# The last expert's rows read back and written plainly in place of accumulated: an attention and mixture-of-experts kernel on one core

## The chip, the cores and the metric

The kernel runs on one core of a Trainium2 chip. The metric is device time in microseconds (us), lower is better. Five engines work side by side: TensorE (PE in the profile, PEld its weight loads), VectorE (DVE), ScalarE (ACT), GpSimd (POOL) and SyncE (SP). Each runs its own instruction stream and waits for the others by semaphores. DMAs are issued here by SyncE and by GpSimd. A PSUM bank holds 128 x 512 float32; DMA can't read one, so results leave a bank through ScalarE or VectorE.

## The reference

```python
def _L0_ffn_ref(hidden_states, gate_weight, gate_up_proj, down_proj):
    ...
    probs = jax.nn.softmax(router_logits.astype(jnp.float32), axis=-1)
    top_v, top_i = jax.lax.top_k(probs, top_k)
    top_v = top_v / top_v.sum(axis=-1, keepdims=True)
    combine_w = jnp.einsum('tke,tk->te', jax.nn.one_hot(top_i, num_experts, dtype=top_v.dtype), top_v).astype(x.dtype)
    def expert_step(acc, inp):
        gu, dp, w = inp
        gate, up = jnp.split(x @ gu.T, 2, axis=-1)
        hidden = jax.nn.silu(gate) * up
        y = hidden @ dp.T
        return (acc + w[:, None] * y, None)
    ...
x = x + _L0_xattn_ref(_layernorm(x, axis=-1), mask_BxSx4224_bf0, ctx_2048, ctx_2048, ...)
x = x + _L0_ffn_ref(_layernorm(x, axis=-1), ...)
```

x has 8 x 112 tokens of 512 numbers. After an attention block each token goes to two of 8 experts with inner width 1024, and the weighted outputs of its two experts are added to it.

## The kernel before, in words

The first 185 us do the attention of the 8 batches in four pairs, write the sum x2 = x + attention to `out`, normalise it, choose two experts for each token and scatter each token's normalised row, with its weight and its number, into a list for each expert in DRAM (`slots`, 256 rows of 514 numbers an expert, unused rows zero). The scatter is an indirect write on GpSimd (L1327): 112 rows of 2,056 bytes, the destination rows given by a column of indices.

Then come the experts, one after another, two to an iteration `it` of a loop (three iterations, then the fourth unrolled with `more=False`). For an expert, `xe` holds its list of 256 rows, and its inner width is done in 8 units of 128. For each unit TensorE does the gate and up products (L412, L413; the last unit in a shorter form, L230 to L234), ScalarE and VectorE form silu(gate) * up and split it into a high and a low part, and TensorE adds the unit's share of the down product (`pe_down`, L498) into two banks `YB[e]` that hold the 256 rows as two halves: SC0 and SC1 for an even expert, R and T2 for an odd one. After the eighth unit the sum is whole, which TensorE signals for each half by `y_mm`.

An expert's output takes this way. ScalarE (`y_out`, L814) multiplies each half by the rows' weights (column D of `xe`) into `ys`, signal `y_ok`. GpSimd (`send_y`, L1362) sends each half by an indirect write with `compute_op=ALU.add`: the DMA adds the 128 rows of 2,048 bytes to rows of `out`. The indices `yidx` are made by VectorE from column D + 1 of `xe` (L1174, L1176, signal `yidx_ok`), in the fifth unit of the expert; unused rows go to spare rows behind the real ones. Between experts GpSimd (`add_y`) waits for both landings (`y_added`) and then sets a flag (`y_free`, L1276) that lets ScalarE write `ys` again. So the adds of one expert never meet those of another.

The kernel can hold longer lists: behind the eighth expert every engine loads the length of the longest list (`value_load`) and skips a large body of code if it is at most 256 (`CAP`). In the profiled execution it is skipped by every engine. On VectorE this test stands directly behind its last operation for the eighth expert (L1220, L1221), on ScalarE behind `y_out` of the last expert (L880, L881), on GpSimd between the seventh expert and the last (L1378, L1379), on TensorE behind its last product (L633, L634), on SyncE behind its last load (L1508). After the body GpSimd does `send_y(NE - 1, 1)` for the eighth expert, and SyncE waits for all of `y_added` (L1536). L45 is not a line of the kernel: it is the end of the program, where every engine has a DRAIN and a handshake.

Of the kernel before, what the change touches and what calls it, by code (L numbers as in the profile page):

```python
# [4 lines left out]
F32 = mybir.dt.float32  # L5
# [5 lines left out]
ALU = mybir.AluOpType  # L11
# [4 lines left out]
D = 512  # L16
# [6 lines left out]
NE = 8  # L23
# [3 lines left out]
ROUNDS = 4  # L27
# [13 lines left out]
def build_kernel(nc, x, ctxT, ctxn, w_all, gwt, units, out):  # L41
# [3 lines left out]
    with stack:  # L45
        def sem(name):
            return stack.enter_context(nc.semaphore(name))
# [6 lines left out]
        def at(name, shape, dt, offset):  # L54
            return nc.alloc_sbuf_tensor_at(name, shape, dt, offset=offset)
# [7 lines left out]
        def sb(name, shape, dt):  # L63
            offset = top[0]
            top[0] += size(shape, dt)
            return at(name, shape, dt, offset)
# [14 lines left out]
        yidx = sb("yidx", [128, 2, 2], I32)  # L81
# [63 lines left out]
        o_e = top[0]  # L145
# [7 lines left out]
        o_l = top[0]  # L153
# [14 lines left out]
        xe = [at(f"xe{n}", [128, 2, RW], F32, o_s + n * 4128) for n in range(2)]  # L168
# [13 lines left out]
        ys = at("ys", [128, 2, D], F32, o_e)  # L182
        hh = [at(f"hh{n}", [128, CAP], F32R, o_e + 4096 + n * 1024) for n in range(2)]
        hl = [at(f"hl{n}", [128, CAP], F32R, o_e + 6144 + n * 1024) for n in range(2)]


        T = [pb(f"T{n}") for n in range(3)]
# [206 lines left out]
        gu_mm, silu_ok, h_ok = sem("gu_mm"), sem("silu_ok"), sem("h_ok")  # L394
        y_mm, y_ok, yidx_ok = sem("y_mm"), sem("y_ok"), sem("yidx_ok")
        y_added, y_free = sem("y_added"), sem("y_free")
        UB = 2 * IT

        LG = 3
# [7 lines left out]
        YB = [[SC[0], SC[1]], [R, T[2]]]  # L407
# [66 lines left out]
        def pe_gu_short(pe, it, u):  # L474


            e = u // IT
            pe.wait_ge(u_lo, it * UB + u + 1)
            wh, wl = uh[u % GU], ul[u % GU]
            for w in range(2):  # L480
                hl_matmul(GB[u % 2][w][:, 0:CAP],
                          lambda k: wh[:, w * D + 128 * k:w * D + 128 * k + 128],
                          lambda k: wl[:, w * D + 128 * k:w * D + 128 * k + 128],
                          lambda k: eh[e][:, k, :], lambda k: el_[e][:, k, :], KT).then_inc(gu_mm if w else g_mm, 1)

        def pe_gu(pe, it, u):
            e = u // IT
            pe.wait_ge(u_lo, it * UB + u + 1)
            if u % IT == 0:
                pe.wait_ge(e_lo, 2 * (2 * it + e) + 2)  # L490
            wh, wl = uh[u % GU], ul[u % GU]
            for w in range(2):
                for k in range(KT):
                    c = slice(w * D + 128 * k, w * D + 128 * k + 128)
                    last = gu_product(GB[u % 2][w], wh[:, c], wl[:, c], eb[e], k)
                last.then_inc(gu_mm if w else g_mm, 1)

        def pe_down(pe, it, u):  # L498
            i = u % IT
            pe.wait_ge(h_ok, it * UB + u + 1)  # L500
            if u == IT:
# [13 lines left out]
        def pe_experts(pe, it, more=True):  # L515


            for u in range(1, UB + 1):
                e, i = u // IT, u % IT
                if u == UB - 1 and not more:  # L520
                    pe_gu_short(pe, it, u)
                elif u < UB:
                    pe_gu(pe, it, u)
# [121 lines left out]
        def _(act):  # L645
# [195 lines left out]
            def experts(it, more=True):  # L841

                for u in range(1, UB + 1):
                    e, i = u // IT, u % IT
                    if u == UB - 1 and not more:
                        silu_short(it, u)
                    elif u < UB:
                        silu(it, u)
                        if more or u + LG < UB:
                            hi_u(it, u + LG)  # L850
                    elif more:
                        silu(it + 1, 0)
                        hi_u(it + 1, LG)
                    if (i == 4 or i == 6) and (more or e == 0):
                        hi_e(2 * (2 * it + e + 1) + 1 + i // 6, (e + 1) % 2, i // 6, YB[(e + 1) % 2][i // 6])
                    if i == 0:
                        y_out(it, e - 1)

            for p in range(PAIRS):
# [19 lines left out]
            act.wait_ge(most_ok, 1)  # L879
            longest = act.value_load(mosti[0:1, 0:1], min_val=0, max_val=TOK)  # L880
            with act.If(longest > CAP):  # L881
                for u in range(LG):
                    hi_u(NE // 2, u)
                hi_e(2 * NE + 1, 0, 0, YB[0][0])
                hi_e(2 * NE + 2, 0, 1, YB[0][1])
                silu(NE // 2, 0)
                hi_u(NE // 2, LG)
                with act.Fori(NE // 2, ROUNDS * NE // 2 - 1) as j:
                    experts(j)
                experts(ROUNDS * NE // 2 - 1, more=False)  # L890

        @block.vector
        def _(dve):
            v = nc.vector
# [272 lines left out]
            def experts(it, more=True):  # L1167
                for u in range(UB):
                    e, i = u // IT, u % IT
                    b = u % 2  # L1170
                    if i == 4:
                        if e == 0:
                            dve.wait_ge(xe_in[0], 16 * (it + 1))
                        link(v.scalar_tensor_tensor(yidt[:, e, :], xe[e][:, :, D + 1], 0.0, padid[:, :],  # L1174
                                                    ALU.is_equal, ALU.mult))
                        v.scalar_tensor_tensor(yidx[:, e, :], xe[e][:, :, D + 1], -1.0, yidt[:, e, :],  # L1176
                                               ALU.add, ALU.add).then_inc(yidx_ok, 1)
                    if u == UB - 1 and not more:
                        dve.wait_ge(gu_mm, it * UB + u + 1)
                        dve.wait_ge(silu_ok, it * UB + u + 1)  # L1180
                        link(v.tensor_tensor(hf[b][:, :], GB[b][1][:, 0:CAP], hs[b][:, :], ALU.mult))
                    else:
                        dve.wait_ge(u_copy, it * UB + u + 1 - short[0])
                        link(v.tensor_tensor(us[b][:, :], GB[b][1][:, 0:CAP], us[b][:, :], ALU.add))
                        dve.wait_ge(silu_ok, it * UB + u + 1)
                        link(v.tensor_tensor(hf[b][:, :], us[b][:, :], hs[b][:, :], ALU.mult))  # L1186
                    link(v.tensor_copy(hh[b][:, :], hf[b][:, :]))
                    v.tensor_tensor(hl[b][:, :], hf[b][:, :], hh[b][:, :].bitcast(F32), ALU.subtract)\  # L1188
                        .then_inc(h_ok, 1)
                    if more or u + LG < UB:  # L1190
                        lo_u(it, u + LG)
                    if u + 1 < UB:
                        if more or u + 2 < UB:
                            sum_g(it, u + 1)
                    elif more:
                        sum_g(it + 1, 0)
                    if (i == 4 or i == 6) and (more or e == 0):
                        lo_e(2 * (2 * it + e + 1) + 1 + i // 6, (e + 1) % 2, i // 6, YB[(e + 1) % 2][i // 6])
# [22 lines left out]
            with dve.If(longest > CAP):  # L1221
                for u in range(LG):
                    lo_u(NE // 2, u)
                lo_e(2 * NE + 1, 0, 0, YB[0][0])
                lo_e(2 * NE + 2, 0, 1, YB[0][1])
                sum_g(NE // 2, 0)
                looped(NE // 2, ROUNDS * NE // 2 - 1, experts)
                experts(ROUNDS * NE // 2 - 1, False)

        @block.gpsimd  # L1230
        def _(pool):
# [130 lines left out]
            def send_y(n, e):  # L1362
                pool.wait_ge(yidx_ok, n + 1)
                for t in range(2):
                    pool.wait_ge(y_ok, 2 * n + 1 + t)
                    pool.indirect_dma_start(out[:, :], bass.IndirectOffsetOnAxis(yidx[:, e, t:t + 1], 0),  # L1366
                                            ys[:, t, :], None, compute_op=ALU.add).then_inc(y_added, 16)

            def add_y(n, e):
                send_y(n, e)  # L1370
                pool.wait_ge(y_added, 32 * n + 32)
                signal(y_free)

            pool.wait_ge(x2_out, 16 * NB + 16 * 2)
            for n in range(NE - 1):
                add_y(n, n % 2)
            pool.wait_ge(most_ok, 1)
            longest = pool.value_load(mosti[0:1, 0:1], min_val=0, max_val=TOK)  # L1378
            with pool.If(longest > CAP):  # L1379
                for n in range(NE - 1, ROUNDS * NE - 1):  # L1380
                    add_y(n, n % 2)

                pool.wait_ge(yidx_ok, ROUNDS * NE)
                pool.wait_ge(y_ok, 2 * ROUNDS * NE)

            send_y(NE - 1, 1)

        @block.sync
        def _(sp):
# [184 lines left out]
```

## Time and profile before

| | |
|---|---|
| runs without the profiler | 456.36, 456.49, 456.56 us; median 456.49 |
| the profiled execution | 456.27 us, of which the span from the first to the last instruction is 454.5 |
| mean granted TensorE clock | 0.994 |
| busy: TensorE, its loads, VectorE, ScalarE, GpSimd | 441.0, 373.3, 343.8, 253.5, 98.7 us |
| instructions | 7156 |
| DMA | 88.39 MB, mean 194 GB/s |

A page of the profile gives each engine's busy time; "idle before" names what ended the idle time. Register, branch, semaphore and DMA-issuing instructions don't count as busy, and stand under an engine's name with a q (DVEq, POOLq). For an indirect DMA, GpSimd is shown busy while it generates the descriptors; the bytes move later. "DMA to landing" runs from the start of that instruction to the last increment of its semaphore. All times are from the span's start.

### The profile page before, as it was taken

The page shows a single profiled execution, that of the slowest core. Times are in us where ns is not written, and L with a number is a line of the kernel's source. Part 1 is how long each engine was busy: PE and PEld are TensorE (multiplying, and loading weights), DVE is VectorE, ACT ScalarE, POOL GpSimd, SP SyncE. Part 2 cuts the span into 40 slices and gives each one's busy share as a digit, 9 for nine tenths or more (in the row PEclk, how much of TensorE's full clock was granted, in tenths as well). Part 3 has the DMA queues.
Part 4 walks back from the last instruction along what each step waited for, and adds up shares of the span by engine and source line. Part 5 has one row for each costly group of instructions (what it writes and reads, how often), then busy time and mean ns, then how long its engine had stood idle before and what let it go on. Part 6 is the DMA issues. An engine that isn't in the chain of part 4 may idle for free.

```text
span 454.5 us, 7156 instructions
## 1 busy us (share of the span) xinstructions
PE 441.0 (97%) x2530; PEld 373.3 (82%) x2530; DVE 343.8 (76%) x644; ACT 253.5 (56%) x414; POOL 98.7 (22%) x128
## 2 busy tenths in 40 slices
PE   8999999999999999999999999999999999999991
PEld 6979888878888678888888888888888888888880
DVE  5867546556645678898988988988988888888850
ACT  4566434514623666666566566666666656656621
POOL 6060071334427253003003003003003003003002
PEclk9999999999999999999999999999999999999997
DMA  8996984434545465976766856856956846856203
GB/s 274 349 259 186 278 216 139 142 51 140 195 115 226 129 224 153 341 236 194 249 199 176 272 185 199 263 165 205 276 156 204 276 157 198 284 164 196 56 0 51
DMA packets 26911, 88.39 MB, mean 194 GB/s; under 512 B 2560, under 2 KB 8704, under 8 KB 26880
## 3 DMA queue, kind: packets, MB, share of 16 engines
q1 hardware_dynamic: 23296, 80.13, 54.4%
q0 software_dynamic: 3584, 7.88, 8.7%
q8 instruction: 16, 0.26, 0.3%
q14 instruction: 15, 0.12, 0.1%
HBM read 73.55 MB, written 14.45 MB: 194 GB/s over the span
## 4 chain that ended last, share of the span: by engine, by line
PE 85%; DVE 4%; DMA 3%; ACT 2%; issue 2%; POOL 1%; SPq 1%; POOLq 0%; ACTq 0%; DVEq 0%
PE T L412 13%; PE PJ L412 13%; PE PJ L413 6%; PE T L413 6%; PE SC L509 3%; PE SC L510 3%; PE SC L511 3%; PE T L245 3%; PE PJ L232 2%; PE PJ L234 2%; PE PJ L233 2%; PE SC L262 2%; PE SC L266 2%; PE SC L264 2%; DMA wTs<-in_weights 2%
## 5 line engine op out<-in xcount | busy, mean ns | idle before, releaser
L897 DVE TENSOR_TENSOR ul<-ng,uh 128x1536 fp32r<-128x1536 f32 x64 | 112.5, 1757 | 3.1 <-ACT uh L647 1.9
L647 ACT ACTIVATE uh<-ng 128x1536 fp32r<-128x1536 f32 x64 | 94.8, 1481 | 0.3 <-DMA ng<-in_units 0.3
L412 PE MATMUL T<-eb,uh 128*128 128x512 f32 x248 | 88.7, 397 | 0.0
L412 PE MATMUL PJ<-eb,uh 128*128 128x512 f32 x248 | 88.7, 397 | 0.0
L1366 POOL DMA_INDIRECT out<-ys,yidx x16 | 27.8, 1738 | 194.3 <-ACT ys L821 191.8
L413 PE MATMUL PJ<-eb,ul 128*128 128x256 f32 x248 | 69.7, 281 | 0.0
L413 PE MATMUL T<-eb,ul 128*128 128x256 f32 x248 | 69.6, 281 | 0.0
L412 PEld LDWEIGHTS PJ<-eb,uh 128*128 128x128 f32 x248 | 46.6, 188 | 11.2
L412 PEld LDWEIGHTS T<-eb,uh 128*128 128x128 f32 x248 | 46.6, 188 | 11.2
L413 PEld LDWEIGHTS T<-eb,ul 128*128 128x128 f32 x248 | 46.8, 189 | 1.3
L413 PEld LDWEIGHTS PJ<-eb,ul 128*128 128x128 f32 x248 | 46.7, 188 | 1.3
L1289 POOL TENSOR_TENSOR vl<-vs,vh 128x512 fp32r<-128x512 f32 (+1 forms) x24 | 30.6, 1308 | 8.0 <-DVE xr L992 5.4
L647 ACT ACTIVATE us<-PJ 128x256 f32<-128x256 f32 x32 | 12.3, 384 | 31.5 <-PE PJ L413 31.4
L1186 DVE TENSOR_TENSOR hf<-us,hs 128x256 f32<-128x256 f32 x63 | 26.8, 425 | 3.0 <-ACT hs L839 1.1
L1188 DVE TENSOR_TENSOR hl<-hf,hh 128x256 fp32r<-128x256 f32 x64 | 27.2, 425 | 2.2
L839 ACT ACTIVATE hs<-gs 128x256 f32<-128x256 f32 x63 | 25.9, 412 | 4.0 <-DVE gs L1165 3.9
L647 ACT ACTIVATE us<-T 128x256 f32<-128x256 f32 x31 | 11.9, 384 | 28.4 <-PE T L413 28.4
L509 PE MATMUL SC<-uh,hh 128*128 128x512 f32 x64 | 25.9, 405 | 0.0
L510 PE MATMUL SC<-ul,hh 128*128 128x512 f32 x64 | 25.2, 393 | 0.0
L511 PE MATMUL SC<-uh,hl 128*128 128x512 f32 x64 | 25.1, 392 | 0.0
L647 ACT ACTIVATE gs<-PJ 128x256 f32<-128x256 f32 x32 | 12.2, 382 | 23.0 <-PE PJ L413 22.0
L1327 POOL DMA_INDIRECT slots<-xr,idx x16 | 17.5, 1095 | 18.8 <-issue 17.3
(240 smaller groups left out, 918.5 us busy)
## 6 DMA issues: line engine op xcount, KB each, us to landing
ng<-in_units SPq DMA_DIRECT2D x64, 768.0 KB, 4.5
vs<-in_ctxn SPq DMA_DIRECT2D x8, 768.0 KB, 5.2
kTs<-in_ctxT SPq DMA_DIRECT2D x8, 750.0 KB, 5.0
slots<-zero SPq DMA_DIRECT2D x8, 514.0 KB, 12.9
xe<-slots SPq DMA_DIRECT2D x8, 514.0 KB, 4.3
wTs<-in_weights SPq DMA_DIRECT2D x8, 512.0 KB, 8.0
out<-x_all SPq DMA_DIRECT2D x8, 224.0 KB, 3.9
x_all<-in_x SPq DMA_DIRECT2D x1, 896.0 KB, 19.0
```

What stands on the lines that cost most here:

```text
L412: nc.tensor.matmul(o[:, :].rearrange("p (h s) -> p h s", h=2), wh, both[:, k, :, :], start=k == 0, stop=False)
L413: return nc.tensor.matmul(o[:, 0:CAP], wl, both[:, k, 0, :], start=False, stop=k == KT - 1)
L509: nc.tensor.matmul(o, hh[b][:, s], wh, start=i == 0, stop=False)
L510: nc.tensor.matmul(o, hh[b][:, s], wl, start=False, stop=False)
L511: last = nc.tensor.matmul(o, hl[b][:, s], wh, start=False, stop=i == IT - 1)
L647: nc.scalar.activation(o, i, ACT.Copy).then_inc(s, 1)
L839: nc.scalar.activation(hs[b][:, :], gs[b][:, :], ACT.Silu).then_inc(silu_ok, 1)
L897: v.tensor_tensor(o, whole, hi.bitcast(F32), ALU.subtract).then_inc(s, 1)
L1186: link(v.tensor_tensor(hf[b][:, :], us[b][:, :], hs[b][:, :], ALU.mult))
L1188: v.tensor_tensor(hl[b][:, :], hf[b][:, :], hh[b][:, :].bitcast(F32), ALU.subtract)\
L1289: g_.tensor_tensor(vl[a][0:n, j, :], vs[a][0:n, j, :], vh[a][0:n, j, :].bitcast(F32), ALU.subtract).then_inc(v_lo, 1)
L1366: pool.indirect_dma_start(out[:, :], bass.IndirectOffsetOnAxis(yidx[:, e, t:t + 1], 0), ys[:, t, :], None, compute_op=ALU.add).then_inc(y_ ...
```

## The change

VectorE takes over the last expert's output. GpSimd reads the rows of `out` that this expert adds to into a new tile `so_far`, once the seven others are added and the indices are there. VectorE computes bank x weight + `so_far` into `ys`, and GpSimd writes the rows by two indirect writes without `compute_op`. ScalarE's `y_out` of the eighth expert moves into the skipped body. If the body runs, it reads `so_far` again at its own end.

```diff
+        so_far = at("so_far", [128, 2, D], F32, o_e + 8192)
...
+        far_in, last_ok = sem("far_in"), sem("last_ok")
...
-                    if i == 0:
+
+                    if i == 0 and (more or e == 1):
                         y_out(it, e - 1)
...
             with act.If(longest > CAP):
+                y_out(NE // 2 - 1, 1)
...
                 experts(ROUNDS * NE // 2 - 1, False)
+                dve.wait_ge(far_in, 64)
+                dve.wait_ge(y_mm, 2 * ROUNDS * NE)
+
+            dve.wait_ge(far_in, 32)
+            for t in range(2):
+                dve.wait_ge(y_mm, 2 * NE - 1 + t)
+                v.scalar_tensor_tensor(ys[:, t, :], YB[1][t][:, :], xe[1][:, t, D:D + 1], so_far[:, t, :],
+                                       ALU.mult, ALU.add).then_inc(last_ok, 1)
...
+            def read_far(n):
+
+                pool.wait_ge(yidx_ok, n)
+                for t in range(2):
+                    pool.indirect_dma_start(so_far[:, t, :], None, out[:, :],
+                                            bass.IndirectOffsetOnAxis(yidx[:, 1, t:t + 1], 0)).then_inc(far_in, 16)
+
             pool.wait_ge(x2_out, 16 * NB + 16 * 2)
             for n in range(NE - 1):
                 add_y(n, n % 2)
+            read_far(NE)
             pool.wait_ge(most_ok, 1)
             longest = pool.value_load(mosti[0:1, 0:1], min_val=0, max_val=TOK)
             with pool.If(longest > CAP):
+                pool.wait_ge(far_in, 32)
                 for n in range(NE - 1, ROUNDS * NE - 1):
                     add_y(n, n % 2)
-
-                pool.wait_ge(yidx_ok, ROUNDS * NE)
-                pool.wait_ge(y_ok, 2 * ROUNDS * NE)
-
-            send_y(NE - 1, 1)
+                read_far(ROUNDS * NE)
+
+            for t in range(2):
+                pool.wait_ge(last_ok, t + 1)
+                pool.indirect_dma_start(out[:, :], bass.IndirectOffsetOnAxis(yidx[:, 1, t:t + 1], 0),
+                                        ys[:, t, :], None).then_inc(y_added, 16)
```

VectorE's listing ends so before the change; L1181 to L1188 are the last unit's work of the eighth expert, and the last row is the jump over the body, which itself stands above these rows in a second copy of the same lines.

```order
L1184 TENSOR_TENSOR us_181<-PJ,us_181 128x256 [waits u_copy]
L1186 TENSOR_TENSOR hf_159<-us_181,hs_157 128x256 [waits silu_ok,vchain]
L1187 CAST hh_184<-hf_159 128x256 [waits vchain]
L1188 TENSOR_TENSOR hl_186<-hf_159,hh_184 128x256 [waits vchain]
L1181 TENSOR_TENSOR hf_160<-T,hs_158 128x256 [waits silu_ok,gu_mm]
L1187 CAST hh_185<-hf_160 128x256 [waits vchain]
L1188 TENSOR_TENSOR hl_187<-hf_160,hh_185 128x256 [waits vchain]
L1221 UNCONDITIONAL_BRANCH
```

With the change it ends so, the lines being 6 higher from there on.

```order
L1192 TENSOR_TENSOR hf_159<-us_181,hs_157 128x256 [waits silu_ok,vchain]
L1193 CAST hh_184<-hf_159 128x256 [waits vchain]
L1194 TENSOR_TENSOR hl_186<-hf_159,hh_184 128x256 [waits vchain]
L1187 TENSOR_TENSOR hf_160<-T,hs_158 128x256 [waits silu_ok,gu_mm]
L1193 CAST hh_185<-hf_160 128x256 [waits vchain]
L1194 TENSOR_TENSOR hl_187<-hf_160,hh_185 128x256 [waits vchain]
L1227 UNCONDITIONAL_BRANCH [waits y_mm,far_in]
L1241 SCALAR_TENSOR_TENSOR ys<-R,xe_156,so_far 128x512 [waits y_mm,far_in]
L1241 SCALAR_TENSOR_TENSOR ys<-T,xe_156,so_far 128x512 [waits y_mm]
L45 UNCONDITIONAL_BRANCH
```

The two new rows stand behind the end of the skipped body. The test itself (COMPARE_AND_BRANCH) is row 503 of the listing in both kernels, and the body ends at row 786 or 787: some 284 rows are jumped over. On ScalarE they are 173, on TensorE some 750.

GpSimd, from the seventh expert's writes to the test, before the change:

```order
L1366 DMA out<-ys,yidx 1152x512 [waits y_ok,yidx_ok]
L1366 DMA out<-ys,yidx 1152x512 [waits y_ok]
L1276 MEMSET flags 1x1 [waits y_added]
L1378 TENSOR_LOAD mosti [waits most_ok]
L1378 ISA x2
L1379 COMPARE_AND_BRANCH
```

and with it:

```order
L1380 DMA out<-ys,yidx 1152x512 [waits y_ok,yidx_ok]
L1380 DMA out<-ys,yidx 1152x512 [waits y_ok]
L1290 MEMSET flags 1x1 [waits y_added]
L1392 DMA so_far<-out,yidx 128x512 [waits yidx_ok]
L1392 DMA so_far<-out,yidx 128x512
L1400 TENSOR_LOAD mosti [waits most_ok]
L1400 ISA x2
L1401 COMPARE_AND_BRANCH
```

Two gathers have come between the seventh expert's flag and the test, behind a wait for the eighth expert's indices.

## Rows read from the trace of the kernel before

**Rows 1.** The page: busy us (share of the span) and instructions of each engine.

```profile
PE 441.0 (97%) x2530; PEld 373.3 (82%) x2530; DVE 343.8 (76%) x644; ACT 253.5 (56%) x414; POOL 98.7 (22%) x128
```

**Rows 2.** Timeline from 443.9: start us, us, engine, line, operation [idle before <-releaser].

```profile
443.99 0.39 PE L511 MATMUL R<-uh,hl 128*128 128x512 f32 x1
...
444.48 0.69 ACT L821 ACTIVATE ys<-R,xe 128x512 f32<-128x512 f32 x1 [3.31 <-PE R L511]
...
445.11 0.69 ACT L821 ACTIVATE ys<-T,xe 128x512 f32<-128x512 f32 x1
445.95 1.56 POOL L1366 DMA_INDIRECT out<-ys,yidx  x1 [21.39 <-ACT ys L821]
447.81 1.54 POOL L1366 DMA_INDIRECT out<-ys,yidx  x1 [0.30 <-issue]
```

**Rows 3.** The chain of waits, its last piece: start us, us, what.

```profile
447.51 1.85 POOLq L45
```

**Rows 4.** L1366 from 445 to 455, the last expert's two writes.

```profile
DMA to landing us min/median/max: 4.7/4.9/5.1
```

**Rows 5.** L45 by engine: duration ns min/median/max, first and last start us.

```profile
L45 POOLq DRAIN  x1: 8093/8093/8093, 446.2 to 446.2; - x1
...
L45 SPq COMPARE_BRANCH  x1: 38/38/38, 452.9 to 452.9; - x1
...
L45 ACTq DRAIN  x1: 81/81/81, 446.4 to 446.4; - x1
...
L45 DVEq DRAIN  x1: 65/65/65, 446.7 to 446.7; - x1
```

**Rows 6.** L981 on VectorE: an SBUF tile added to a bank.

```profile
L981 DVE TENSOR_TENSOR x_all<-PJ,x_all x7: 680/691/692, 48.6 to 157.3; 112x512 f32<-112x512 f32 x7
```

**Rows 7.** The jumps over the body: VectorE, TensorE, ScalarE.

```profile
L1221 DVEq COMPARE_BRANCH  x1: 63/63/63, 443.9 to 443.9; - x1
...
L634 PEldq COMPARE_BRANCH  x1: 3561/3561/3561, 444.3 to 444.3; - x1
...
L881 ACTq COMPARE_BRANCH  x1: 54/54/54, 445.9 to 445.9; - x1
```

**Rows 8.** VectorE's loop branch, and the operation behind it in the timeline.

```profile
L1203 DVEq COMPARE_BRANCH  x3: 50/56/72, 239.3 to 377.3; - x3
...
239.76 0.42 DVE L1165 TENSOR_TENSOR gs<-PJ,gs 128x256 f32<-128x256 f32 x1
```

**Rows 9.** L1327, plain indirect writes: one at 169.6 with its landing; four from 147.1.

```profile
L1327 POOL DMA_INDIRECT slots<-xr,idx x1: 1068/1068/1068, 169.6 to 169.6; - x1
...
DMA to landing us min/median/max: 3.4/3.4/3.4
...
L1327 POOL DMA_INDIRECT slots<-xr,idx x4: 937/942/1056, 147.1 to 150.9; - x4
...
DMA to landing us min/median/max: 3.9/4.8/5.1
```

**Rows 10.** L1460 on SyncE, direct plain writes of zeros to out, 161.8 and 162.3.

```profile
DMA to landing us min/median/max: 2.6/2.8/3.1
```

**Rows 11.** The last indices (L1176); GpSimd's timeline behind expert seven; landing of its writes.

```profile
L1176 DVE SCALAR_TENSOR_TENSOR yidx<-xe,yidt x8: 160/161/161, 188.9 to 429.7; 128x2 int32<-128x2 f32 x8
...
418.37 1.66 POOL L1366 DMA_INDIRECT out<-ys,yidx  x1 [0.30 <-issue]
424.47 0.09 POOL L1276 MEMSET flags<- 1x1 f32 x1 [4.45 <-DMA out<-ys,yidx]
...
DMA to landing us min/median/max: 6.1/6.5/6.9
```

**Rows 12.** All of L1327; landings of all of L1366; SyncE's last loads.

```profile
L1327 POOL DMA_INDIRECT slots<-xr,idx x16: 937/944/2215, 85.8 to 174.7; - x16
...
DMA to landing us min/median/max: 4.7/8.5/10.7
...
L1447 SPq DMA_DIRECT2D ng<-in_units x3: 328/328/328, 407.8 to 416.7; - x3
```

More of the change, by code:

```diff
@@ L184, in build_kernel @@
         hl = [at(f"hl{n}", [128, CAP], F32R, o_e + 6144 + n * 1024) for n in range(2)]
+        so_far = at("so_far", [128, 2, D], F32, o_e + 8192)
+        assert o_e + 12288 <= o_l
         T = [pb(f"T{n}") for n in range(3)]
```

## Prediction

> **What bounds the kernel now.** I read the page first: TensorE is busy 441.0 of 454.5 us [rows 1], so until its last product nothing that this change touches can matter unless it holds TensorE up. Then I looked at what happens after that product, in the timeline of the end [rows 2]. The last product into R starts at 443.99, ScalarE scales R into the first half of ys at 444.48 and T into the second at 445.11 (0.69 each). GpSimd generates the first accumulating write at 445.95 (1.56 us) and the second at 447.81 (1.54 us). The chain of waits ends in GpSimd's queue at L45, the end of the program [rows 3]. The issue-to-landing times of the two writes are 4.7 and 5.1 us [rows 4], so the first lands at 450.6 and the second at 447.81 + 5.1 = 452.9. At L45 [rows 5], SyncE's wait for the landing is over at 452.9, but GpSimd's DRAIN lasts from 446.2 for 8.093 us, to 454.3, and is the last thing to end: 1.4 us behind the landing, 4.9 us behind the end of the second generation (449.35). The tail from the scaled ys to the end of the span is thus a bit over 9 us, and it is all that the change can shorten.
>
> **The change part by part.** The sum is made against the profiled execution, whose span is 454.5 and whose time is 456.27; the median of the three runs shown is 456.49, so a change of the span is added to that median.
>
> *Who scales the last rows.* ScalarE's two ys instructions of the last expert go, two of VectorE come (bank times weight plus so_far). The nearest row is VectorE's add of a bank and an SBUF tile, 112x512, 690 ns [rows 6]; ScalarE took 687 ns [rows 2]. So the operation itself is worth 0. ScalarE has nothing else to do there.
>
> *When VectorE can start.* This is the term that decides. The new instructions stand behind VectorE's test on the longest list. It already exists: the branch at L1221 starts at 443.9 [rows 7], before R is complete. But it is taken over the whole overflow body, 284 rows of the listing, and VectorE's next instruction behind it, the DRAIN at L45, starts only at 446.7 [rows 5]. It waits for nothing that the trace shows, and ScalarE's own DRAIN, behind the same sort of test but a shorter body, starts 0.5 us behind its branch (445.9 to 446.4) [rows 5, 7]. So I read 446.7 - 443.9 = 2.8 us as the price of the long jump. In the changed kernel the first instruction behind the jump is the one that everybody waits for: it starts at about 446.8, not at 444.48. That costs **+2.3 us**. The bounds: 0.3 to 0.5 us of delay from the branches that go on quickly (VectorE's loop branch at 239.3, whose next operation runs at 239.76 [rows 8], and ScalarE's); and 3.6 us from TensorE's branch at L634, which starts at 444.3 and is shown 3561 ns long [rows 7]. I take 2.8, because it is this engine's jump over this body. From the quick end the start is bound by R, at 444.5, and the term is 0; from the slow end it is 443.9 + 3.6 + 0.1 = 447.6, +3.1.
>
> *The hand-over.* ScalarE's first half ends at 445.17 and GpSimd starts at 445.95, 0.78 us later. The same wait stands in the new kernel for last_ok: 0. The first write is then issued at 446.8 + 0.69 + 0.78 = 448.3. VectorE's second half ends at about 448.15, before GpSimd is free for it.
>
> *Generating the writes.* From the first generation to the second the accumulating ones took 447.81 - 445.95 = 1.86 us. A plain indirect write of 112 rows took 1.07 us as the first of its batch and 0.94 in the median of four [rows 9]; with the 0.30 us between two of them that is 1.36 instead of 1.86, **-0.5 us**. Bounds: 0.94 + 0.3 (-0.6), and no gain at all (0), if 128 rows cost as an accumulating write does.
>
> *From the second generation to its landing.* It was 5.1 us. The plain indirect write that ran alone landed 3.4 us behind its issue, those of a batch of four beside loads in 3.9 to 5.1 [rows 9]; two direct plain writes of 256 KB each landed in 2.6 to 3.1 [rows 10]. At the end of the program nothing else runs, and the first write will be all but through when the second is generated, so I take a value close to the lone one, 3.5: **-1.6 us**. Bounds: 2.6 (-2.5) and 4.5 (-0.6). The Trainium skill, "DMA: Bandwidth & Descriptors", section "Anatomy of one DMA — SWDGE (gpsimd) path", fits such a transfer by 2.0 us plus bytes over 436 GB/s; for 262,144 bytes that is an estimate of 2.6 us, and the sum by it would be 0.9 us lower than mine. The lone plain write of 112 rows, a smaller one, needed 3.4 here, so the trace speaks against it.
>
> *The end.* GpSimd's DRAIN ends 1.4 us behind the landing, as now: 0.
>
> *The reading back.* Two gathers, 256 KB each, come on GpSimd's queue. Behind which wait? They need the indices of the last expert, which VectorE writes at 429.7 [rows 11], and nothing is queued behind them but the test and the last two writes. GpSimd had put the seventh expert's flag at 424.47 [rows 11] and was idle from there to 445.95. There is no gather in this trace; the dearest indirect DMA of any sort took 2.2 us to generate, and the slowest landing, of an accumulating one, was 10.7, with a median of 8.5 [rows 12]. With 430.0 + 2.2 + 0.3 + 10.7 the rows are there by 443.2, and by 441 with the median landing. VectorE wants them at 446.8. At the cheap end they cost nothing either. The loads of the experts' weights are over by then (SyncE issues the last at 416.7 [rows 12]), so they disturb no transfer and are not disturbed. GpSimd's own test, now right behind 424.5, moves behind the gathers, to about 434; even with 3.6 us for its jump it is waiting by 438. If this cover were gone, each microsecond that so_far is late would be one on the end. 0. Releasing ys: with the last expert written by VectorE, the wait for y_free at its head goes; it was long satisfied.
>
> **The sum**: +2.3 - 0.5 - 1.6 = +0.2 us. 456.49 + 0.2 = **456.7 us**. The change does what it should (the writes are cheaper by 2.1 us), and the jump takes it back. Its own range: the landing's bounds alone give -0.7 to +1.2, the slow end of the stall alone +1.0, a stall of half the size -1.2. That is 455.3 to 457.7.
>
> **The rivals.**
>
> *A, VectorE goes on at once.* The 2.8 us could belong to the DRAIN or to the end of the program and not to the jump, so that the new instructions run when R is ready, at 444.5. For it: the loop's branches cost 0.3 to 0.5 us [rows 8]. Against it: ScalarE's DRAIN at the same L45 came at once, TensorE's branch shows 3.6 us of its own. Then the first term is 0: -0.5 - 1.6 = -2.1, **454.4 us**, faster. The Trainium skill, "Runtime: NRT & Kernel Launch", section "Instruction fetch mechanics", says that a taken branch stalls only if its target lies outside a window of two pages of 256 instructions, and forces the fetch of a page otherwise. A target 284 rows on may lie in such a window, in which case this rival would be right; ScalarE's 173 rows cost 0.5 us and agree with the rule, and VectorE's 2.8 speaks for the other side of it.
>
> *B, slower: GpSimd's DRAIN counts from the last generation, not from the landing.* It ended 4.9 us behind the end of the second generation and 1.4 us behind the landing, and this trace has only this one, so it can't tell which. SyncE's wait was over at 452.9, and the DRAIN is what the span ended on. If what it does behind the last generation takes 4.9 us whatever lands, the cheaper landing is worth nothing. The second generation then ends at 448.3 + 1.36 + 1.0 = 450.7 instead of 449.35, **+1.3 us, 457.8 us**. It decides as soon as those 4.9 us end later than the landing and its 1.4, which here is so for any landing quicker than 4.5 us behind the issue. Against it: in the loop the flag of the seventh expert is set at 424.47, and its second write, issued at 418.37, lands 6.1 us later, at 424.47 as well [rows 11]; so GpSimd is free for the next thing long before 4.9 us are over, and a DRAIN that asks for the landed state of the queues is the plainer reading.
>
> *C, the change doesn't do what it says:* the gathers or GpSimd's test come so late that the last writes wait for so_far. It needs a landing beyond 446.8, 14 us behind the second gather's issue; the slowest in the trace is 10.7. By that it would be 457 to 460.
>
> **How the numbers follow.** A difference of 0.2%, 0.9 us, is about what a measurement of this kernel can tell from none. The forecast gets 0.62 (0.50 within 0.2%, 0.04 faster with a stall of half the size or less, 0.08 slower with TensorE's stall or a landing of 4.5). A gets 0.16, all faster. B gets 0.18, 0.16 of it slower and 0.02 within. C and the like get 0.04, slower. So 0.20 faster, 0.52 the same, 0.28 slower. The range takes in the forecast's own, a stall of half the size (-1.2, 455.3) and B: 455.0 to 457.9. Left out are A and C.
>
> **What would show it.** In the changed profile: VectorE's first scalar_tensor_tensor starts near 446.8, 2.8 us behind its branch, and TensorE's last product near 444 as before; the two so_far gathers start near 430 and land before 443; GpSimd's last two writes start at 448.3 and 449.6, take 1.0 us each and land in 3.4 to 3.6; the DRAIN ends 1.4 us behind the landing. A start at 444.5 makes A right, a DRAIN that ends 4.9 us behind the last generation B. The forecast is wrong also if the plain writes of 128 rows to out take as long as the accumulating ones: then it is +2.3.

## The result, and the profile after

The changed kernel takes 455.16 us in the median of 22 runs, the kernel before 456.26 us in the median of its runs beside them; the ratio is 0.998, with a 95% interval of 0.9971 to 0.999. So it is faster by 0.2%, a little over 1 us. The profiled execution is at 455.30 us with a span of 453.5, 1.0 us less than before. I had forecast 456.7, and no difference, from a sum of +0.2 us. Two terms of the sum, both of which I had carried over from a row that stood near, were too dear by 0.5 and 0.8 us; the others came within 0.1 us. One execution each of e10 (734.05 us) and of e12 (546.96 us), far off the others, is left out of their ratios.

The timeline of the end, to be read beside [rows 2] (start us, us, engine, line, operation, idle before and what ended it):

```profile
443.93 0.40 PE L515 MATMUL R<-uh,hl 128*128 128x512 f32 x1
...
446.81 0.75 DVE L1241 SCALAR_TENSOR_TENSOR ys<-R,xe,so_far 128x512 f32<-128x512 f32 x1 [3.52 <-issue]
447.48 0.74 DVE L1241 SCALAR_TENSOR_TENSOR ys<-T,xe,so_far 128x512 f32<-128x512 f32 x1
447.85 0.99 POOL L1409 DMA_INDIRECT out<-ys,yidx  x1 [15.34 <-DVE ys L1241]
449.14 0.98 POOL L1409 DMA_INDIRECT out<-ys,yidx  x1 [0.30 <-issue]
```

R is complete as early as before, but VectorE starts on it only at 446.81. The idle time is not put down to an engine or a DMA ("issue"), and the chain of waits shows where it lies, between the branch and the next wait:

```profile
443.80 0.06 DVEq L1227
443.86 2.87 issue
446.73 0.02 DVEq L1240
```

At L45, answering to [rows 5], and the landings of L1409, answering to [rows 4]:

```profile
L45 POOLq DRAIN  x1: 5047/5047/5047, 448.3 to 448.3; - x1
L45 SPq COMPARE_BRANCH  x1: 38/38/38, 451.9 to 451.9; - x1
...
DMA to landing us min/median/max: 2.7/3.0/3.2
```

GpSimd's DRAIN ends at 453.3, 1.4 us behind SyncE's wait for the landing, just as before, and it is still the last thing to end. The reading back is where it was meant to be:

```profile
L1392 POOL DMA_INDIRECT so_far<-out,yidx x2: 1018/1070/1122, 430.1 to 431.4; - x2
```

Term by term; the first two columns are from the profiled executions, in us, and the last two say by how much the change moves the end:

| | before | changed | change, forecast | change, measured |
|---|---|---|---|---|
| the scaling starts | 444.48 | 446.81 | +2.3 | +2.33 |
| one half takes | 0.69 | 0.75 | 0 | +0.06 |
| its end to the first write's start | 0.78 | 0.28 | 0 | -0.50 |
| first write to second | 1.86 | 1.30 | -0.5 | -0.56 |
| second write to its landing | 5.1 | 2.7 | -1.6 | -2.4 |
| landing to the DRAIN's end | 1.4 | 1.4 | 0 | 0 |
| sum | | | +0.2 | -1.1 |

### The profile page after: what moved, and what is told of

Its sections match the earlier page's. It is cut to its first block, busy times and chain, and to the rows that moved or that the text cites. A ratio compares the mean times of both kernels' runs of the same rounds, so it can differ in the third digit from the quotient of the medians.

```text
span 453.5 us, 7157 instructions
## 1 busy us (share of the span) xinstructions
PE 441.0 (97%) x2530; PEld 373.4 (82%) x2530; DVE 345.8 (76%) x646; ACT 251.9 (56%) x412; POOL 99.8 (22%) x130
## 4 chain that ended last, share of the span: by engine, by line
PE 85%; DVE 5%; issue 3%; DMA 2%; ACT 2%; POOL 1%; POOLq 0%; DVEq 0%
PE T L416 13%; PE PJ L416 13%; PE PJ L417 6%; PE T L417 6%; PE SC L513 3%; PE SC L514 3%; PE SC L515 3%; PE T L248 3%; PE PJ L235 2%; PE PJ L237 2%; PE PJ L236 2%; PE SC L265 2%; PE SC L269 2%; PE SC L267 2%; DMA slots<-xr,idx 2%
## 5 line engine op out<-in xcount | busy, mean ns | idle before, releaser
L1380 POOL DMA_INDIRECT out<-ys,yidx x14 | 24.7, 1766 | 171.5 <-ACT ys L825 169.3
L1190 DVE TENSOR_TENSOR us<-PJ,us 128x256 f32<-128x256 f32 x32 | 13.6, 424 | 10.9 <-ACT us L651 10.9
```

## The experiments

Ratios are to the kernel before, measured beside each; the changed kernel's is 0.998.

**e1: VectorE's results ahead of its test.** They go to a tile of their own, `fin`, which the two last writes now send, so that the skipped body, if it runs, can make them again.

```diff
+        fin = at("fin", [128, 2, D], F32, o_e + 12288)
...
+            def finish(read, made):
+                dve.wait_ge(far_in, read)
+                for t in range(2):
+                    dve.wait_ge(y_mm, made - 1 + t)
+                    v.scalar_tensor_tensor(fin[:, t, :], YB[1][t][:, :], xe[1][:, t, D:D + 1], so_far[:, t, :],
+                                           ALU.mult, ALU.add).then_inc(last_ok, 1)
+
+            finish(32, 2 * NE)
             longest = dve.value_load(mosti[0:1, 0:1], min_val=0, max_val=TOK)
             with dve.If(longest > CAP):
...
+                finish(64, 2 * ROUNDS * NE)
...
             with pool.If(longest > CAP):
-                pool.wait_ge(far_in, 32)
+                pool.wait_ge(last_ok, 2)
...
                 read_far(ROUNDS * NE)
+                pool.wait_ge(last_ok, 4)
```

> VectorE's two new instructions stand ahead of its test on the longest list, and write a tile of their own (fin), so nothing is jumped over before them; if the body runs it computes them again. Theory (the 2.9 us between branch and first new instruction are the price of the jump over the body): the first starts when R is complete, about 444.5 instead of 446.8, GpSimd's first write about 445.6 instead of 447.8, and the time falls 2.2 to 2.4 us below the changed kernel's 455.2, to about 452.9. Rival (the instructions wait for something else that comes at 446.8, the rows read back or the banks): the start stays at 446.8 and the time at 455.2.

Measured: 454.02 us, ratio 0.9942 (0.9923 to 0.9961). The timeline:

```profile
444.49 0.75 DVE L1232 SCALAR_TENSOR_TENSOR fin<-R,xe,so_far 128x512 f32<-128x512 f32 x1 [1.14 <-PE R L516]
...
445.52 0.99 POOL L1413 DMA_INDIRECT out<-fin,yidx  x1 [12.96 <-DVE fin L1232]
446.82 0.98 POOL L1413 DMA_INDIRECT out<-fin,yidx  x1 [0.31 <-issue]
```

The start is at 444.49, released by TensorE, so the 2.3 us were the jump's, and both writes go 2.3 us earlier. But the time fell by 0.4%, some 1.7 us, and in the profiled execution (455.2 us, the slowest of its nine) the span is 453.4, hardly less than the changed kernel's. The landing says why:

```profile
DMA to landing us min/median/max: 3.3/4.1/5.0
```

The second write took 5.0 us again instead of 2.7. A write's landing is told in 16 increments of its semaphore, which I read as one share for each of the core's 16 DMA engines. Of the second write's 16 shares 15 had told of their landing by 449.55; the last did at 451.77. This opened a question that the prediction hadn't asked, and e5, e6 and e12 go after it.

**e2: one wait at the write instead of two.** The kernel before, with a tiny memset that takes the wait for the indices.

```diff
             def send_y(n, e):
                 pool.wait_ge(yidx_ok, n + 1)
+                if n == NE - 1:
+                    signal(rest_ready)
```

> The kernel before, with one tiny GpSimd memset between the wait for the last indices and the last expert's first write, so that the write has only one wait left (for ys). Theory (GpSimd starts an indirect DMA 0.28 us behind a signal when that is the DMA's only wait, and 0.78 when a separate wait instruction stands ahead of it): first write 0.5 us earlier, about 445.45, time 0.5 us below the kernel before. Rival (0.28 against 0.78 lies in who signals, VectorE or ScalarE, or in the accumulating form): the write still starts 0.78 behind ScalarE's end and the time is unchanged.

```profile
444.99 0.69 ACT L822 ACTIVATE ys<-T,xe 128x512 f32<-128x512 f32 x1
445.32 1.56 POOL L1369 DMA_INDIRECT out<-ys,yidx  x1 [15.43 <-ACT ys L822]
```

ScalarE's first half starts at 444.36 and ends at 445.05; the write starts 0.28 us later, although ScalarE signals and the write accumulates. So the hand-over is a matter of the waits at the DMA and not of who signals: with two, one of them stands as an instruction of its own (L1365 in the kernel before) and the DMA is dispatched only behind it. In the trace the whole 0.5 us is there. The time is 456.53, ratio 0.9995 (0.998 to 1.001), too wide an interval to show 0.1%; that the 0.5 us reach the end is read from the profiled spans alone, 453.9 against 454.5.

**e3: the changed kernel, its last writes still accumulating.** What was read back is then counted twice.

```diff
-                                        ys[:, t, :], None).then_inc(y_added, 16)
+                                        ys[:, t, :], None, compute_op=ALU.add).then_inc(y_added, 16)
```

> The changed kernel with compute_op=ALU.add left on its last two writes, so the last expert's rows of the output are counted twice over. Theory (the plain form alone saves 0.56 us between the generations and 2.4 us from the second issue to the landing): 2.9 us slower than the changed kernel, 458.1, each generation about 1.55 us, landing of the second 5.1 behind its issue, hand-over still 0.28. Rival (the landing was quicker because it fell later, in a quieter time): within 0.6 us of 455.7. And GpSimd's DRAIN: if it follows the landing it ends 1.4 us behind it, if it follows the generation it ends 3.2 us behind the second generation, as in the changed kernel.

Measured: 458.81 us, ratio 1.0041 (1.0023 to 1.0059), 0.6% or 2.8 us above the changed kernel. The generations:

```profile
448.79 1.61 POOL L1409 DMA_INDIRECT out<-ys,yidx  x1 [15.52 <-DVE ys L1241]
450.70 1.57 POOL L1409 DMA_INDIRECT out<-ys,yidx  x1 [0.30 <-issue]
```

and the landings and the end:

```profile
DMA to landing us min/median/max: 4.9/5.0/5.2
...
L45 POOLq DRAIN  x1: 8097/8097/8097, 449.2 to 449.2; - x1
L45 SPq COMPARE_BRANCH  x1: 38/38/38, 455.9 to 455.9; - x1
```

The form alone is worth what the theory said (2.9 us), and the hand-over of 0.28 stays (448.51 to 448.79). The DRAIN ends at 457.3, 1.4 us behind the landing but 5.0 behind the second generation's end, where the changed kernel had 3.2: it follows the landing.

**e4 and e10: a shorter body to jump over.** e4 leaves the last unrolled iteration out of VectorE's skipped body (188 rows of the listing are left), e10 nearly all of it (4 rows are left).

```diff
                 sum_g(NE // 2, 0)
                 looped(NE // 2, ROUNDS * NE // 2 - 1, experts)
-                experts(ROUNDS * NE // 2 - 1, False)
                 dve.wait_ge(far_in, 64)
```

```diff
-                lo_e(2 * NE + 1, 0, 0, YB[0][0])
-                lo_e(2 * NE + 2, 0, 1, YB[0][1])
-                sum_g(NE // 2, 0)
-                looped(NE // 2, ROUNDS * NE // 2 - 1, experts)
-                experts(ROUNDS * NE // 2 - 1, False)
                 dve.wait_ge(far_in, 64)
```

> The changed kernel with the last unrolled iteration of VectorE's skipped body left out (lists over 256 are no longer handled; the body doesn't run with these inputs). The jump goes over some 190 rows of the listing instead of 284, near ScalarE's 173 that cost 0.5 us. Theory A (it is the distance that costs: the target has to lie near enough): first new instruction about 0.5 us behind the branch or when R is ready, 444.5, time near 452.9. Theory B (every forward jump of VectorE costs this): still 446.8, time 455.2.

> The changed kernel with all but the three first subtractions and the last waits left out of VectorE's skipped body (lists over 256 are no longer handled). The jump goes over about ten rows. Theory A (a near target is already in the engine's own memory, a far one has to be fetched): VectorE goes on 0.3 to 0.5 us behind its branch, the first new instruction starts when R is ready, 444.5, and the run behaves as e1, median about 454.0, with a straggling share. Theory B (any taken forward branch at this place costs it): first new instruction at 446.8 as in e4, time of the changed kernel.

e4, branch and new instruction:

```profile
L1227 DVEq COMPARE_BRANCH  x1: 63/63/63, 444.0 to 444.0; - x1
...
L1240 DVE SCALAR_TENSOR_TENSOR ys<-R,xe,so_far x1: 751/751/751, 447.0 to 447.0; 128x512 f32<-128x512 f32 x1
```

e10:

```profile
L1227 DVEq COMPARE_BRANCH  x1: 63/63/63, 443.5 to 443.5; - x1
...
L1236 DVE SCALAR_TENSOR_TENSOR ys<-R,xe,so_far x1: 753/753/753, 444.2 to 444.2; 128x512 f32<-128x512 f32 x1
```

Over 188 rows the new instruction starts 3.0 us behind the branch, as over 284 (e4: 455.85 us, ratio 0.9977, 0.9959 to 0.9994, as the changed kernel). Over 4 VectorE goes on 0.6 us behind its branch and then waits for R alone (e10: 454.77 us, ratio 0.9959, 0.9943 to 0.9975). So e4 came out by its theory B and e10 by its theory A: a near target costs little, and between 188 and 284 rows the cost doesn't grow. ScalarE jumped over 173 rows in 0.5 us. Where the limit lies, and whether it is a number of rows or the place of the target in the engine's code, was not tried.

**e7: the plain writes alone.** The kernel before, without `compute_op` on the last two writes; the last expert's rows then hold its share alone.

```diff
-            send_y(NE - 1, 1)
+            send_y(NE - 1, 1, {})
```

(`send_y` passes its last argument on in place of `compute_op=ALU.add`.)

> The kernel before with the last expert's two writes made plain, and nothing else: ScalarE scales, nothing is read back, so the last expert's rows of the output hold only its own share. ScalarE's halves and GpSimd's first write stay at 444.48 and 445.95 (hand-over 0.78). Theory (the plain form saves 0.56 us between the generations and about 2.4 from issue to landing): second write at 447.25, landing 2.7 behind it, 449.95, unless TensorE's fetch at 448.5 holds one share up as in e1, then about 451.8. Time 453.4 without, 455.1 with the hold-up. Rival (the landing was short for another reason, the later time): landing still 4.5 to 5.1 in all shares.

Measured: 455.07 us, ratio 0.9968 (0.9956 to 0.9979); writes at 445.68 and 446.98, 0.82 us behind ScalarE's end, and

```profile
DMA to landing us min/median/max: 3.4/3.8/4.3
```

15 shares of the second write landed by 449.71 and the last at 451.27. The case with the hold-up came, with the time named for it (455.1); the late share came at 451.3 where I had named 451.8.

**e5, e6 and e12: TensorE's instruction fetches.** The trace's DMA records hold packets of instructions, too. From 443 on (start + length in us, bytes):

```
before   444.89+0.51 8192   445.29+1.01 16384   446.99+0.40 8192    447.35+0.47 8192   450.10+0.95 16384
changed  444.82+0.54 8192   445.22+1.10 16384   447.32+0.36 8192    448.46+1.01 16384
e1       445.28+1.04 16384  447.05+0.50 8192    448.49+1.82 16384   449.51+0.36 8192
e5       447.17+0.54 8192   447.25+1.91 16384   449.60+0.40 8192    451.33+1.12 16384
e6       447.31+0.59 8192   449.74+0.43 8192
e12      444.97+0.55 8192   447.58+0.55 8192
e7       444.59+0.51 8192   444.99+1.01 16384   446.70+0.42 8192    447.02+0.60 8192   448.28+1.51 16384
e10      444.95+1.28 16384  445.60+0.31 8192    449.15+0.93 16384
e4       445.08+0.42 8192   445.47+1.30 16384   447.52+0.47 8192    448.92+1.31 16384
```

A packet of 8,192 bytes follows VectorE's branch by 1.0 us in every kernel of this table but e10 (the branch is at 443.9, 443.8 and 446.0 in the first three), and VectorE goes on 1.2 to 1.5 us behind its end. In e10, with the near target, VectorE is already past its branch when the next such packet starts. The first 16,384 follow TensorE's branch (444.3, 444.2 and 444.3 in the first three) by 1.0. In e1 the second 16,384 are one packet, from 448.49 to 450.31, right across the second write. The records don't name a packet's DMA engine, but they show the queueing: all but the last share's packets of that write are over by 449.20, and the four of the last one start at 450.29, as the fetch ends. In e7 the same four start at 449.78, and its fetch ends at 449.79. The next three kernels test it: e6 is e1 without TensorE's test and body; e12 is the changed kernel without them; e5 is e1 with this line ahead of TensorE's test:

```diff
+            pe.wait_ge(last_ok, 1)
             longest = pe.value_load(mosti[0:1, 0:1], min_val=0, max_val=TOK)
```

> The kernel of e1 without TensorE's test and its body of some 750 rows (lists over 256 are no longer handled; not needed with these inputs). Theory (TensorE's instruction fetches are what holds one share up): no 16 KB instruction packet near 448.5, all 16 shares of the second write land within 0.1 us of each other near 449.55, span about 451.2, time 452.9 with little spread. Rival (another cause): one share lands near 451.8 again, median 454.0.

> The kernel of e1 (VectorE's results ahead of its test), and TensorE waits for the first of them before its own test. Theory (in e1 15 of 16 shares of the second write had landed by 449.55 and the last only at 451.77, because 16 KB of instructions that TensorE fetches 0.6 us after it goes on behind its jump, at 448.5, occupied one DMA engine until 450.3): TensorE's branch moves from 444.3 to about 446.1, its fetches to about 447.1 and 450.2, the second write lands whole by about 449.6 to 449.9, the span ends near 451.3 and the time is 453.0 to 453.3. Rival (the straggling share has another cause, DRAM for instance): one share still lands 2 us late, median near e1's 454.0.

> The changed kernel without TensorE's test and body. Theory (because VectorE starts 2.3 us late, its writes pass behind TensorE's fetch of 16 KB at 448.5, which holds up at most shares of the first write; the second lands 2.7 us behind its issue either way): the first write's last two shares come in 0.5 us earlier, and the end, set by the second, moves by less than 0.2 us, unless VectorE's own fetch is quicker without TensorE's beside it. Rival (the fetch costs the changed kernel too): over 0.5 us faster.

e6: 453.33 us, ratio 0.9929 (0.9909 to 0.9949), four runs from 453.18 to 453.76, span 451.5. Its page counts two instruction packets fewer in this queue, q8, than the 16 of every kernel with TensorE's jump, and the shares of its second write land from 449.64 to 449.82:

```profile
q8 instruction: 14, 0.23, 0.2%
```

```profile
DMA to landing us min/median/max: 2.7/3.0/3.3
```

So the straggling share came from TensorE's fetch, and what e1 lost by it in its profiled execution is 1.9 us of span. The medians don't separate the two kernels: e1's interval and e6's overlap. e5: 454.19 us, ratio 0.9951 (0.9933 to 0.9969), no better than e1. TensorE's branch moved to 446.3 and the fetch to 447.25, but it took 1.91 us beside the first write, and one share of each write came behind it, at 450.65 and 451.26, where I had expected 449.6 to 449.9. Theory right, its size wrong: a packet of 16 KB and the writes slow each other. e12: 455.95 us, ratio 0.9977 (0.9957 to 0.9997), as the changed kernel:

```profile
L1399 POOL DMA_INDIRECT out<-ys,yidx x2: 985/991/997, 448.1 to 449.4; - x2
...
DMA to landing us min/median/max: 2.7/2.7/2.8
```

The first write's last share, 0.5 us behind the others in the changed kernel (451.08 against 450.60), comes with them here, and the second needs 2.7 as before. In the profiled execution of the changed kernel the fetch costs nothing, because VectorE's late start has pushed the second write behind it; in e4, which starts as late, the last share lands 0.25 us behind the others (452.32 against 452.07).

**e8: the gathers alone.** The kernel before with both gathers and a wait for them ahead of GpSimd's test.

```diff
+            pool.wait_ge(yidx_ok, NE)
+            for t in range(2):
+                pool.indirect_dma_start(so_far[:, t, :], None, out[:, :],
+                                        bass.IndirectOffsetOnAxis(yidx[:, 1, t:t + 1], 0)).then_inc(far_in, 16)
+            pool.wait_ge(far_in, 32)
             pool.wait_ge(most_ok, 1)
```

> The kernel before, with the two gathers of the last expert's rows added where the change has them and waited for ahead of GpSimd's test; nothing uses them. Theory (they lie in GpSimd's idle time, 424.5 to 445.9, and cost nothing): both land by 436, the test follows, the last writes start as before and the time is that of the kernel before within 0.3 us. Rival (they disturb the experts or come late): a later end of TensorE's products or a later first write.

456.75 us, ratio 0.9996 (0.9978 to 1.0013). They land 3.3 to 3.6 us behind their issue, and GpSimd's branch, behind the wait for them, is at 436.1:

```profile
L1386 POOLq COMPARE_BRANCH  x1: 53/53/53, 436.1 to 436.1; - x1
```

Nothing is left of them at 446. No cost of the reading back is seen, within the 0.2% that this interval allows.

**e9: loads beside the plain writes.** The changed kernel; SyncE sends four loads of 768 KB when VectorE's first half is done.

```diff
+            sp.wait_ge(u_lo, NE * IT)
+            sp.wait_ge(last_ok, 1)
+            for n in range(NG):
+                load_u(0, n, n)
             sp.wait_ge(y_added, 32 * NE)
+            for n in range(NG):
+                sp.wait_ge(u_in[n], 16 * (NE * IT // NG + 1))
```

> The changed kernel, in which SyncE issues four loads of 768 KB (weights that nobody uses) as soon as VectorE's first half is done, so that the two plain writes go out beside traffic; their landing is waited for too, which makes the run longer, so only the writes' own landing is read. Theory (the plain write of the attention part needed 3.4 us and more because loads and TensorE's work ran beside it, and 2.7 is what it needs alone): the writes land 3.4 to 5 us behind their issue. Rival (it is the form, 128 rows of 2,048 bytes in packets of 4,096 against 112 rows of 2,056): still 2.7 to 3.2.

```profile
L1409 POOL DMA_INDIRECT out<-ys,yidx x2: 985/990/996, 449.0 to 450.3; - x2
...
DMA to landing us min/median/max: 7.9/8.1/8.3
...
L45 POOLq DRAIN  x1: 10609/10609/10609, 449.4 to 449.4; - x1
```

A single execution, 463.6 us, the loads' landing included. The same writes, the same rows, three times the landing: traffic can move it, and by more than I had expected. It doesn't follow that traffic made the 3.4 of [rows 9]. The DMA records show that the last load packet beside that write was over at 171.30, when the write's own had only begun (171.20 to 172.55), and its shares landed from 172.21 to 172.93, that is 2.7 to 3.4 us behind the issue. The first share was as quick as here; why the last ones came later is open. The DRAIN ends at 460.0, 1.4 us behind the landing at 450.26 + 8.3 = 458.6, and 8.7 behind the generation.

## Why the prediction was wrong

The forecast was "the same" by a sum of +0.2, and the kernel is 0.2% faster. Step by step:

- *When VectorE can start*, +2.3: right to 0.03 us. I took the time from VectorE's own DRAIN behind the jump, and the new instruction stood exactly there. e1 and e10 show that it is the jump, and rival A is dead. By the rule of the Trainium skill, "Runtime: NRT & Kernel Launch", section "Instruction fetch mechanics", a taken branch to a target outside the two pages that the engine holds costs a fetch. That a far target costs a fetch and a near one doesn't, e1, e4 and e10 agree with. The size that the Trainium skill gives, 256 instructions to each of the two pages, doesn't fit VectorE here: the target 188 rows of the listing on cost 3.0 us in e4, behind a packet of 8,192 bytes.
- *Who scales*, 0: 0.75 instead of 0.69, a small miss.
- *The hand-over*, 0: **failed, by 0.5 us.** I read 0.78 us between ScalarE's end and GpSimd's start as the price of a signal to GpSimd. It belonged to the second wait at that DMA, for indices that had been there for 15 us (e2). The new write has one wait. I had given this term no bounds. The row from which it could have been seen was at hand: the wait at L1365 stands as its own instruction at 445.2, while ScalarE's end is at 445.17.
- *Generating*, -0.5: right (-0.56).
- *Landing*, -1.6: **failed, mis-sized by 0.8 us.** Right that a plain write lands quicker (e3, e7), but I priced it by the lone plain write of the attention part, 3.4 us, and took 3.5. Behind the last product a plain write takes 2.7 (the second write of e6, e12 and the changed kernel). The 3.4 was the last share of a write in the middle of the program; e9 shows that traffic can make a write land later, but what held those shares up is not shown. The estimate by the fit of the Trainium skill, "DMA: Bandwidth & Descriptors", section "Anatomy of one DMA — SWDGE (gpsimd) path", 2.6 us, was the nearer one: the sum by it was -0.7. I set it aside on that one row, measured under other conditions.
- *The end*, 0: right. Rival B is dead: the DRAIN ended 1.4 us behind the landing in the changed kernel, e3 and e9, but 3.2, 5.0 and 8.7 us behind the second generation.
- *The reading back*, 0: right (e8). The rows are there by 435.3 (the second gather is issued at 431.4 and the slower landing takes 3.9), 11.5 us before VectorE wants them; rival C is dead. GpSimd's test didn't even wait for the gathers: its branch is at 430.7, where I had put the test at 434.

With 0.28 and 2.7 in their places the sum is -1.1. Both failures were in the same direction, and each alone would have left the difference under 0.2%. That 455.16 lies inside the range of 455.0 to 457.9 is luck: the low end was put there for a stall of half the size, which didn't happen, and not for a cheaper hand-over and landing.

The version that comes out of it is e1: the results ahead of the test, 454.02 us, ratio 0.9942, below both kernels with intervals that don't meet. e6 has the lower median, 453.33, not clear of e1's, and gives up long lists.

## What to carry to other kernels

An instruction put behind a jump over a long body waits for the jump, so put what ends the program ahead of such a test, and look for the cost beforehand in the first instruction that each engine runs behind its jump. Price a transfer by a row measured in the same conditions, and a hand-over by a row with the same number of waits at the waiting instruction. When a tail has been shortened, look at the single shares of its last DMA: something small on one DMA engine can hold it up.

## What I had not expected

A DMA on GpSimd with one wait starts 0.28 us behind the signal and with a second wait, long satisfied, 0.78 to 0.82. TensorE, once it has gone on behind its jump, fetches another 16 KB, 0.7 to 2.7 us later, which nobody waits for. A packet of 16 KB took 0.9 to 1.9 us, and it delayed one share in 16 of the last write by 1.6 to 2.2 us (e1, e7, e10; in e5 it was the jump's own packet). VectorE's 8,192 bytes seem to do the same on a small scale: in e6 they pass from 447.31 to 447.90, and one share of the first write lands 0.5 us behind the others. The late start of VectorE, which costs the changed kernel 2.3 us, saved it from this in its profiled execution. That undoing it (e1) gave 1.7 us in the median and nearly nothing in one execution fits this, but a trace was read for that one execution alone.
